# Three products of zeros added to z after each couple's sums in a graph layer kernel

## The chip, the cores and the metric

The kernel runs on one core of one Trainium2 chip. The metric is the device time of one execution in microseconds (us). The reader needs five of the core's engines: TensorE (PE in the rows, with PEld for its weight loads), VectorE (DVE), ScalarE (ACT), GpSimd (POOL, which here issues the gathers) and SyncE (SP, which issues the other DMAs).

## What is computed

The reference is one message-passing layer on a graph of 12500 nodes and 200000 edges, the edges sorted by their destination:

```python
h = jnp.maximum(_layernorm(x, axis=-1), 0.0)            # 12500 x 64
e = jnp.concatenate([h[src], h[dst]], axis=1)           # 200000 x 128
m = jax.nn.relu(e @ W1 + b1) @ W2 + b2                  # 200000 x 64
s = jax.ops.segment_sum(m, dst, num_segments=12500)
cnt = segment_sum(ones, dst)
out = x + s / jnp.maximum(cnt, 1.0)[:, None]
```

## The kernel before

A first stage of about 205 us makes two tables in DRAM: `p_table` holds the source half of `e @ W1` for each node, `q_table` the destination half plus `b1`. The second stage, `fast()`, goes over the edges. 512 edges are a quad; the first 28 quads, whose edges go to few nodes, are done in another way (below); the other 363 are taken two at a time, in 182 couples.

For a couple m, with the edges on the partitions in chunks of 128:

- POOL gathers the 1024 rows of `p_table` by `src` into a ring of 26 quads of the tile `g`, 128 rows to an indirect DMA (`gather`, L672, 8 for a couple). Before each fourth quad it waits for the semaphore `u_psum`, which counts the couples whose sums are done (L670). How many quads it may run ahead falls in five steps from 26 to 8, by 4 each 48 quads (L669, the last step by 2); at a step it has to wait for more couples than usual.
- PE puts the q rows of the edges' nodes into `z`, a PSUM tile of 128 x 1024 float32 (`spread_q`, L1374, 8 products of 128 columns), and adds the gathered rows by a product with the identity (`add_rows`, L1386, 2 products of 512 columns). Float32 products stand as two records each in the trace.
- ACT takes the relu of z back into g (`relu`, L812), which tells PE by `r_done`.
- PE sums the edges by node (`sum_edges`, L1401, 8 products of 128 columns, the last of which raises `u_psum`).
- Every couple or two `times_w2` turns the counts (L1408) and multiplies by W2 (L1419); `turn_batch` (L1430, 4 products) turns the sums of a batch of nodes, 25 times in all. DVE adds the results (L1100) and makes the means.

z is there once, so `spread_q(m + 1)` waits for the relu of m. The order on PE in the loop over m is add_rows(m), times_w2 of an earlier couple, dense(m), spread_q(m+1), sum_edges(m). `dense` is the work for the first 28 quads: six tallies a couple (L1445, bfloat16) in the couples 3 to 42, then, from couple 49 on, products of DVE on PSUM (L1153, some 7 to a couple, which read the other PSUM tile `turned`), with eight transposes on PE at the start of each of 13 spans of about 10 couples (`turn_p`, L1461).

I call a round the time from the start of one batch of 16 gathers on POOL to the start of the next; it covers two couples.

Of the kernel before, what the change touches and what calls it, by code (L numbers as in the profile page):

```python
# [14 lines left out]
NODES, FEAT, HID, EDGES = 12500, 64, 128, 200000  # L15
# [34 lines left out]
COUPLES = -(-(QUADS - Q0) // 2)  # L50
# [16 lines left out]
def couple(m):  # L67
    return range(Q0 + 2 * m, min(Q0 + 2 * m + 2, QUADS))
# [24 lines left out]
def groups_to(k):  # L93

    return sum(len(p) for p in BLOCKS[:k])
# [111 lines left out]
def gnn_kernel(nc, x, src, dst, W1, b1, W2, b2, out):  # L207
# [6 lines left out]
    with ctx:  # L214
        def sb(name, shape, dt=F32):
            return ctx.enter_context(nc.sbuf_tensor(name, shape, dt))
# [8 lines left out]
        ident = sb("ident", [128, 128])  # L225
# [3 lines left out]
        zeros = sb("zeros", [128, 128])  # L229
# [111 lines left out]
        z, turned = z_all  # L341
# [69 lines left out]
        def chunks_of(n):  # L411
            return CHUNKS - 4 * n if n == QUADS - 1 else 4
# [19 lines left out]
        def slot(n):  # L432
            return (n - Q0) % RING
# [815 lines left out]
        def _(pe):  # L1249
# [92 lines left out]
            for of, to in ((span, bank[1]), (worst, bank[2])):  # L1342
                for t in range(QT):
                    last = nc.tensor.matmul(to[0:1, 128 * t:128 * (t + 1)], of[:, t:t + 1], ident[:, :],
                                            start=True, stop=True)
# [17 lines left out]
            def spread_q(m):  # L1363

                pe.wait_ge(spread_done, parts_to(m + 1))
                if m:
                    pe.wait_ge(r_done, m)
                for n in couple(m):
                    i = GROUP[n]
                    if n == GROUPS[i][0]:  # L1370
                        pe.wait_ge(window_in[i % WINDOWS], 16 * (i // WINDOWS + 1))
                    for c in range(chunks_of(n)):
                        at = 512 * (n % 2) + 128 * c
                        last = nc.tensor.matmul(z[:, at:at + HID], spreads[m % 2][:, at:at + 128],  # L1374
                                                qw[i % WINDOWS], start=c == 0, stop=False)
                last.then_inc(zq_done, 1)
# [13 lines left out]
            def sum_edges(m):  # L1390


                pe.wait_ge(r_done, m + 1)
                if m < MEMBER_FROM:
                    pe.wait_ge(m_made, m + 1)
                k = BLOCK[m]
                for n in couple(m):
                    i = GROUP[n]
                    at = WIN * BLOCKS[k].index(i)
                    for c in range(chunks_of(n)):  # L1400
                        last = nc.tensor.matmul(u_bank[k % 2][:, at:at + WIN], g[:, slot(n), HID * c:HID * (c + 1)],  # L1401
                                                member[:, m % 2, 4 * (n % 2) + c, :], start=n == GROUPS[i][0] and c == 0,
                                                stop=n == GROUPS[i][-1] and c == chunks_of(n) - 1)
                last.then_inc(u_psum, 1)

            def turn_counts(v, parts, at):
                for j in parts:
                    nc.tensor.matmul(v[FEAT:FEAT + 1, at:at + WIN], count[:, j % COUNTS:j % COUNTS + 1], ident[:, :],  # L1408
                                     start=j == parts[0], stop=j == parts[-1])
# [12 lines left out]
            def turn_sums(i):  # L1422

                b = ORDER[i]
                if 0 < i < BATCHES - 1:
                    pe.wait_ge(mean_done, i)
                for j in range(BT):
                    t = BT * b + j
                    first = 2 * NP * (t // 2) + t % 2
                    last = nc.tensor.matmul(o_of(i)[:, j, :], sums[:, first:first + 2 * NP - 1:2], fold[:, :],  # L1430
                                            start=True, stop=True)
                last.then_inc(o_psum, 1)
# [57 lines left out]
            def fast():  # L1490
                spread_q(0)
                def turn_batch(i):
                    pe.wait_ge(v_done, groups_to(MEAN_BLOCK[ORDER[i]] + 1))
                    if ORDER[i] == 0:
                        pe.wait_ge(dense_added, 1)
                    turn_sums(i)

                for m in range(COUPLES):
                    add_rows(m)
                    if m >= 2 and m - 2 == BLOCK_END[BLOCK[m - 2]]:  # L1500
                        times_w2(BLOCK[m - 2])
                    dense(m)
                    if m + 1 < COUPLES:
                        spread_q(m + 1)
                    sum_edges(m)
                    for i in range(BATCHES):
                        if MEAN_AT[i] == m:
                            turn_batch(i)
                assert BLOCK_END[-2:] == [COUPLES - 2, COUPLES - 1]
                for k in (len(BLOCKS) - 2, len(BLOCKS) - 1):  # L1510
                    times_w2(k)
                for i in range(BATCHES):
                    if MEAN_AT[i] >= COUPLES:
                        turn_batch(i)

            def general():
# [25 lines left out]
                for i in range(BATCHES):  # L1542
                    turn_sums(i)

            if_one_window(pe, fast, general)


# [20 lines left out]
```

## Time and profile before

| | before |
|---|---|
| median of 3 runs | 2845.76 us (2832.94 to 2848.27) |
| the profiled execution | 2839.25 us, its span 2837.4 us |
| mean granted TensorE clock | 0.749 of 2.4 GHz |
| busy: PE, DVE, POOL, ACT | 55%, 50%, 48%, 42% of the span |

The span is the time from the first to the last instruction; 1.85 us of the execution lie around it. No engine is busy for much more than half of the span, so the waits between engines have to be read, not the busy times.

### The profile page before, as it was taken

How to read it: one execution, taken by the hardware profiler on the slowest of the kernel's cores; microseconds unless marked ns; L12 is line 12 of the kernel's file. 1: busy time of each engine (PE TensorE's matmuls, PEld its weight loads, DVE VectorE, ACT ScalarE, POOL GpSimd, SP SyncE). 2: the span in 40 equal slices, each digit the busy share in tenths (PEclk: the TensorE clock that was granted, in tenths of full speed). 3: DMA queues.
4: the chain of work that ended last, by engine and by line, in shares of the span. 5: the costliest groups of instructions: out<-in, count | busy, mean ns of one | idle time of the engine just before them, and what ended most of it. 6: DMA issues, size and time to landing. Idle time of an engine off the chain costs nothing.

```text
span 2837.4 us, 26976 instructions
## 1 busy us (share of the span) xinstructions
PE 1548.3 (55%) x8249; PEld 1183.2 (42%) x8250; DVE 1428.9 (50%) x3051; ACT 1189.8 (42%) x2414; POOL 1372.7 (48%) x1460
## 2 busy tenths in 40 slices
PE   1656565566465564455544555455455545555556
PEld 0545353444344443344433444344344434434444
DVE  3554343343324665456655666456565556655421
ACT  1223343444314544345444454344344444444444
POOL 6345545445555445444554435545544554554553
PEclk6878777788787777677776777767776777776778
DMA  4532222222134656556565566556565665665541
GB/s 90 163 109 60 59 61 59 60 59 58 58 98 144 202 181 189 167 169 200 179 192 154 178 188 200 186 159 183 184 192 168 186 191 174 183 186 157 174 119 43
DMA packets 258990, 408.46 MB, mean 144 GB/s; under 512 B 45128, under 2 KB 118749, under 8 KB 258841
## 3 DMA queue, kind: packets, MB, share of 16 engines
q1 hardware_dynamic: 211845, 312.84, 35.7%
q0 software_dynamic: 46432, 93.61, 12.5%
q8 instruction: 68, 1.11, 0.2%
q14 instruction: 81, 0.66, 0.1%
q10 hardware_dynamic: 564, 0.23, 0.0%
HBM read 388.12 MB, written 18.38 MB: 143 GB/s over the span
## 4 chain that ended last, share of the span: by engine, by line
PE 48%; issue 36%; another core or an unknown queue 9%; DVE 6%; ACT 1%; DMA 0%; DVEq 0%; SPq 0%; ACTq 0%
PE z L1374 16%; PE bank L1401 12%; PE z L1386 10%; DVE g L1153 4%; PE bank L1419 2%; PE bank L1408 2%; PE z L1445 2%; PE bank L1430 1%; PE z L1461 1%; DVE rows_b L936 1%; PE bank L1268 1%; DVE norms L920 1%; PE z L1268 1%; ACT g L812 0%
## 5 line engine op out<-in xcount | busy, mean ns | idle before, releaser
L672 POOL DMA_INDIRECT g<-p_table,src_e x1403 | 1326.1, 945 | 1425.3 <-PE bank L1401 960.5
L1153 DVE SCALAR_TENSOR_TENSOR g<-z,norms,g 128x1024 bf16<-128x1024 f32 (+1 forms) x884 | 1019.1, 1214 | 43.5 <-issue 25.3
L812 ACT ACTIVATE g<-z 128x1024 f32<-128x1024 f32 x182 | 185.6, 1020 | 1468.0 <-remote 1153.5
L1100 DVE TENSOR_TENSOR acc<-acc,bank 65x128 f32 x191 | 54.2, 284 | 1201.0 <-remote 1069.7
L1374 PE MATMUL z<-work 128*128 128x128 f32 x1464 | 258.8, 348 | 514.2 <-issue 482.9
L1374 PE MATMUL z<-w,work 128*128 128x128 f32 x1438 | 251.9, 345 | 484.3 <-issue 443.8
L1374 PEld LDWEIGHTS z<-work 128*128 128x128 f32 x1464 | 240.3, 256 | 546.0 <-issue 541.7
L1374 PEld LDWEIGHTS z<-w,work 128*128 128x128 f32 x1438 | 234.4, 253 | 512.3 <-issue 509.3
L1401 PE MATMUL bank<-work,g 128*128 128x128 f32 x2902 | 423.4, 307 | 15.4 <-issue 15.1
L1401 PEld LDWEIGHTS bank<-work,g 128*128 128x128 f32 x2902 | 414.1, 227 | 16.8 <-issue 16.7
L1386 PE MATMUL z<-g,ident 128*128 128x512 f32 x726 | 350.8, 605 | 5.8 <-issue 5.7
L803 ACT ACTIVATE work<-columns,rel_e 128x128 f32<-128x128 f32 x1059 | 324.2, 396 | 0.0
L1386 PEld LDWEIGHTS z<-g,ident 128*128 128x128 f32 x726 | 126.0, 194 | 98.7 <-issue 98.7
L796 ACT ACTIVATE work<-work 128x1024 f32<-128x1024 f32 (+1 forms) x168 | 146.5, 872 | 4.2
L808 ACT ACTIVATE work<-work 128x1024 f32<-128x1024 f32 (+1 forms) x133 | 140.0, 1053 | 4.2
L825 ACT ACTIVATE g<-g,norms 128x512 bf16<-128x512 f32 x157 | 108.3, 716 | 0.0
L1445 PE MATMUL z<-g 128*125 128x512 bf16 x236 | 65.6, 409 | 70.6 <-remote 67.3
L1419 PE MATMUL bank<-sums_u,w 128*64 128x128 f32 (+1 forms) x312 | 78.7, 326 | 33.3 <-issue 33.3
L830 ACT ACTIVATE g<-g 128x512 bf16<-128x512 bf16 x157 | 93.5, 620 | 0.0
L1408 PE MATMUL bank<-ident,count 128*1 128x128 f32 x432 | 74.5, 273 | 9.5 <-issue 9.4
L1408 PEld LDWEIGHTS bank<-ident,count 128*1 128x1 f32 x432 | 23.4, 81 | 128.3 <-issue 125.2
L788 ACT ACTIVATE work<-rel_q,rows_f 128x1024 f32<-128x1024 bf16 (+1 forms) x67 | 75.3, 1124 | 0.0
(161 smaller groups left out, 1063.6 us busy)
## 6 DMA issues: line engine op xcount, KB each, us to landing
g<-tally_table SPq DMA_DIRECT2D x816, 256.0 KB
rel_q<-rel_table SPq DMA_DIRECT2D x46, 512.0 KB
rows_b<-rel_table SPq DMA_DIRECT2D x45, 512.0 KB
g<-p_table,src_e POOLq DMA_INDIRECT x1403
g<-tally_table SPq DMA_DIRECT2D x68, 128.0 KB
work<-q_table SPq DMA_DIRECT2D x96, 64.0 KB
w<-q_table SPq DMA_DIRECT2D x96, 64.0 KB
g<-p_table SPq DMA_DIRECT2D x12, 512.0 KB
```

What stands on the lines that cost most here:

```text
L672: nc.gpsimd.indirect_dma_start(out=g[:, slot(n), j * HID:(j + 1) * HID], out_offset=None, in_=p_table, in_offset=bass.IndirectOffsetOnAxis ...
L796: nc.scalar.activation(to, to, ACT.Relu, bias=1.0, scale=-1.0, accum_out=count[:, j:j + 1])\
L803: last = nc.scalar.activation(member[:, m % 2, c, :], columns[:, :], ACT.Abs, bias=rel_e[:, NC + 8 * m + c:NC + 8 * m + c + 1], scale=-1.0)
L808: nc.scalar.activation(to, to, ACT.Relu, bias=1.0, scale=-1.0)
L812: nc.scalar.activation(rows_of_p(m), z[:, 0:HID * chunks_in(m)], ACT.Relu).then_inc(r_done, 1)
L1153: nc.vector.scalar_tensor_tensor(product[i % BUFFERS][:, 0:w], turned[:, 0:w], minus_q[:, d:d + 1], tally_row[i % BUFFERS][:, 0:w], ALU.ma ...
L1374: last = nc.tensor.matmul(z[:, at:at + HID], spreads[m % 2][:, at:at + 128], qw[i % WINDOWS], start=c == 0, stop=False)
L1386: last = nc.tensor.matmul(z[:, 512 * (n % 2):512 * (n % 2) + w], ident[:, :], g[:, slot(n), 0:w], start=False, stop=True)
L1401: last = nc.tensor.matmul(u_bank[k % 2][:, at:at + WIN], g[:, slot(n), HID * c:HID * (c + 1)], member[:, m % 2, 4 * (n % 2) + c, :], start ...
L1408: nc.tensor.matmul(v[FEAT:FEAT + 1, at:at + WIN], count[:, j % COUNTS:j % COUNTS + 1], ident[:, :], start=j == parts[0], stop=j == parts[-1])
L1419: nc.tensor.matmul(v_of(k)[0:FEAT, 0:w], w2[:, :], sums_u[:, k % 2, 0:w], start=True, stop=True).then_inc(v_psum, 1)
L1445: last = nc.tensor.matmul(tally_bank[i % 2][0:125, :], high_hot[p % TALLY_PLACES], low_hot[p % TALLY_PLACES], start=p == TALLY_FIRST[i], s ...
```

## The change

After `sum_edges(m)` PE makes up to three products of 512 columns that add zeros to z, which at that point holds the q part of couple m+1: the moving operand is one column of the tile `zeros`, read 512 times, the stationary one the identity. They neither wait for nor raise a semaphore of their own. Behind the last but one couple, whose successor has one quad of three chunks, they are two products of 384 columns; behind the last there are none.

```diff
+            def add_nothing(m):
+                if m + 1 == COUPLES:
+                    return
+                for k in range(3):
+                    at = 512 * (k % 2)
+                    w = min(512, HID * chunks_of(couple(m + 1)[k % 2])) if k % 2 < len(couple(m + 1)) else 0
+                    if w:
+                        nc.tensor.matmul(z[:, at:at + w], ident[:, :], zeros[:, 0:1].to_broadcast([128, w]),
+                                         start=False, stop=False)
...
                     if m + 1 < COUPLES:
                         spread_q(m + 1)
                     sum_edges(m)
+                    add_nothing(m)
                     for i in range(BATCHES):
                         if MEAN_AT[i] == m:
                             turn_batch(i)
```

PE's instructions of two couples in the stage with tallies, before. For each: q part into z (L1374), sums (L1401), gathered rows of the next couple into z (L1386), then tallies (L1445) or counts and W2 (L1408, L1419).

```order
L1374 MATMUL z<-w,work 128x128 x8
L1401 MATMUL bank<-work,g 128x128 x8
L1386 MATMUL z<-g,ident 128x512 x2
L1445 MATMUL z<-g 125x512 x6
L1374 MATMUL z<-w,work 128x128 x8
L1401 MATMUL bank<-work,g 128x128 x8
L1386 MATMUL z<-g,ident 128x512 x2
L1408 MATMUL bank<-ident,count 1x128 x2
L1419 MATMUL bank<-sums_u,w 64x128
```

Two such couples on PE after the change; lines behind the new function have numbers that are 10 higher.

```order
L1374 MATMUL z<-w,work 128x128 x8
L1401 MATMUL bank<-work,g 128x128 x8
L1413 MATMUL z<-zeros,ident 128x512 x3
L1386 MATMUL z<-g,ident 128x512 x2
L1455 MATMUL z<-g 125x512 x6
L1374 MATMUL z<-w,work 128x128 x8
L1401 MATMUL bank<-work,g 128x128 x8
L1413 MATMUL z<-zeros,ident 128x512 x3
L1386 MATMUL z<-g,ident 128x512 x2
L1418 MATMUL bank<-ident,count 1x128 x2
L1429 MATMUL bank<-sums_u,w 64x128
```

The zeros (L1413) stand between the sums and the gathered rows of the next couple; nothing else has moved, on this engine or another.

## Rows read from the trace of the kernel before

**Rows 1.** The page: totals, slices, and shares of the chain that ended last.

```profile
PE 1548.3 (55%) x8249; PEld 1183.2 (42%) x8250; DVE 1428.9 (50%) x3051; ACT 1189.8 (42%) x2414; POOL 1372.7 (48%) x1460
...
PEclk6878777788787777677776777767776777776778
...
PE 48%; issue 36%; another core or an unknown queue 9%; DVE 6%; ACT 1%; DMA 0%; DVEq 0%; SPq 0%; ACTq 0%
```

**Rows 2.** Waits, all engines: waiter, releaser, us in total, times, longest.

```profile
ACT g L812 <- remote: 1153.5, 83, 15.6
POOL g L672 <- PE bank L1401: 960.5, 84, 27.9
```

**Rows 3.** Timeline, 1500 to 1560: start, length, what; [idle before].

```profile
1503.90 0.94 POOL L672 DMA_INDIRECT g<-p_table,src_e  x1 [11.01 <-PE bank L1401]
...
1508.36 1.95 PE L1401 MATMUL bank<-work,g 128*128 128x128 f32 x16
1510.15 1.88 PE L1386 MATMUL z<-g,ident 128*128 128x512 f32 x4
...
1512.27 0.43 PE L1419 MATMUL bank<-sums_u,w 128*64 128x128 f32 x2
...
1522.62 0.94 POOL L672 DMA_INDIRECT g<-p_table,src_e  x1 [0.30 <-issue]
1526.70 1.02 ACT L812 ACTIVATE g<-z 128x1024 f32<-128x1024 f32 x1 [14.50 <-remote]
...
1527.82 3.75 PE L1374 MATMUL z<-w,work 128*128 128x128 f32 x16 [15.12 <-issue]
1531.37 2.96 PE L1401 MATMUL bank<-work,g 128*128 128x128 f32 x16
1534.60 0.94 POOL L672 DMA_INDIRECT g<-p_table,src_e  x1 [11.03 <-PE bank L1401]
...
1536.08 1.02 ACT L812 ACTIVATE g<-z 128x1024 f32<-128x1024 f32 x1 [2.56 <-PE z L1386]
1537.20 2.02 PE L1374 MATMUL z<-w,work 128*128 128x128 f32 x16 [0.49 <-issue]
```

**Rows 4.** Windows: sum, busy of PE, PEld, DVE, ACT, POOL, clock, DMA, GB/s.

```profile
1516.00:1519.00 3.00, 0.00 (x0) 0.00 (x0) 0.00 (x0) 0.00 (x0) 2.09 (x4) 0.57 0.81 273
1527.00:1531.00 4.00, 3.18 (x15) 3.21 (x16) 3.54 (x6) 3.97 (x11) 0.00 (x0) 0.50 0.16 53
```

**Rows 5.** Timeline of PE and POOL, a round with eight L1461 and L1430 records more.

```profile
998.84 0.94 POOL L672 DMA_INDIRECT g<-p_table,src_e  x1 [10.97 <-PE bank L1401]
...
1005.39 0.88 PE L1430 MATMUL bank<-fold,acc 65*125 65x65 f32 x6
...
1015.87 0.45 PE L1419 MATMUL bank<-sums_u,w 128*64 128x128 f32 x1 [0.37 <-issue]
...
1029.55 0.94 POOL L672 DMA_INDIRECT g<-p_table,src_e  x1 [11.05 <-PE bank L1401]
```

**Rows 6.** POOL's waits for the sums, 230 to 900, and the start of one batch.

```profile
POOL g L672 <- PE bank L1401: 215.1, 22, 24.6
...
841.28 0.94 POOL L672 DMA_INDIRECT g<-p_table,src_e  x1 [3.49 <-remote]
```

**Rows 7.** The same from 960 to 2800, and the starts of batches behind two steps of the lead.

```profile
POOL g L672 <- PE bank L1401: 684.2, 59, 25.7
...
1701.64 0.94 POOL L672 DMA_INDIRECT g<-p_table,src_e  x1 [24.45 <-PE bank L1401]
2077.24 0.94 POOL L672 DMA_INDIRECT g<-p_table,src_e  x1 [17.77 <-PE bank L1401]
```

**Rows 8.** Timeline: a restart of PE after a short pause, and the clock there (windows).

```profile
853.14 2.77 PE L1374 MATMUL z<-work 128*128 128x128 f32 x16 [3.67 <-issue]
...
853.00:854.00 1.00, 0.86 (x8) 0.89 (x9) 0.00 (x0) 1.00 (x2) 0.70 (x2) 1.00 0.11 29
```

**Rows 9.** Timeline of PE: the end of the program.

```profile
2825.01 0.81 PE L1386 MATMUL z<-g,ident 128*128 128x384 f32 x2
```

## The prediction

> **What bounds the kernel now.** I read the page first. No engine is busy for much over half of the span, and the chain that ended last is 48% PE and 36% "issue", time in which an engine waits for nothing that the profile shows [rows 1]. So the waits decide. They say that two engines wait for each other: POOL waits for PE's sums for 960.5 us in 84 waits, and ACT's relu waits for z for 1153.5 us in 83 [rows 2].
>
> The timeline shows how that can be [rows 3]. Take the round that starts on POOL at 1503.90. The last of its 16 gathers is issued at 1522.62 and ends at 1523.56. ACT's relu starts at 1526.70, 3.14 later, PE's q part at 1527.82, the sums at 1531.37, and the next batch at 1534.60. So a round is 19.66 (gathers) + 3.14 + 1.12 (relu) + 3.55 (q part) + 3.23 (sums) = 30.70 us, for two couples.
>
> What is the relu waiting for? The product that it needs, L1386, has its record at 1510.15, 1.88 long, so it seems done at 1512.03, yet the relu begins 14.67 us later. In the next couple, right after a batch has started, the same relu follows promptly: PE's sums are in by about 1534.3 and the relu starts at 1536.08. I read this so: from about 3 us after a batch starts until 3.1 us after its last gather, PE's records run on, but what PE has done is told to the others only slowly, and the rest in one go at the end. Where the delay sits I can't see; that ACT calls its releaser "remote" only says that the profile has no better name. Call the couple whose sums start a batch A and the one behind it B. A's q part and sums lie in the open, between the landing and the next batch. B's are all issued by 1512.70 (the row of 1512.27 with its 0.43), and PE then idles for 15.12 us. The clock has fallen meanwhile: 0.57 in 1516 to 1519, 0.50 in 1527 to 1531 [rows 4]. So A's q part takes 3.75 us for its 16 records where B's takes 2.02, and its sums 2.96 where B's take 1.95 [rows 3].
>
> **The price of the zeros.** Two products of 512 columns are four records in 1.88 us at the high clock [rows 3]; three are 2.8, less the overlap of their ends; I take 2.7. At the low clock it would be twice as much, 5.4. With 182 couples all of them in the open would cost 180 x 2.7 = 490 us at the high clock, 970 at the low one; nothing if all are covered. They use no other engine and raise no semaphore, so only PE's own order matters: what comes behind them is `add_rows` of the next couple, and behind that its relu.
>
> *A's zeros.* They stand behind `u_psum`, so the batch at 1534.60 doesn't wait for them. `add_rows` ends at 1538.7 instead of 1536.0. That lies past the 3 us in which PE is heard at once, so the relu may come another 1 to 3 us later, and B's q part starts about 1541 to 1543 instead of 1537.20.
>
> *B's zeros.* B's work then ends 2.7 + 2.7 + (1 to 3) = 6.4 to 8.4 us later than before: 1512.70 becomes 1519.1 to 1521.1 in the round shown. The relu is not released before 1526.70 anyway, so 5.6 to 7.6 us are left. The cover is POOL's batch; with it gone each round would cost the 5.4. A natural trial is in the trace: the round from 998.84 has eight L1461 records and eight L1430 records more, is issued only by 1016.3 (1015.87 + 0.45), 17.5 us after its start instead of 8.8, and the next batch still starts at 1029.55, 30.71 us after it [rows 5]. So from 960 on, where 56 of the 59 waits are of one kind, (684.2 - 25.7 - 24.5 - 17.8) / 56 = 11.0 us each [rows 7], I cost the zeros at nothing, but for some five rounds in which they meet both L1461 and L1430: 5 us in all, bounds 0 and 15 (three us each).
>
> *The clock.* With the zeros PE is idle for 15.12 - 6.4 to 8.4 = 6.7 to 8.7 us before the restart. Before, the clock was at half speed by 1519, 6.3 us after the last record [rows 4]. So it has fallen again before A's q part, and A costs what it did. A warm restart exists: at 853.14, after 3.67 us of idling, the clock reads 1.00 and the q part takes 2.77 [rows 8]. The pause would have to shrink to something like that.
>
> **What is not covered.** (a) At a step of POOL's lead two more couples (at the last step one) have to be summed with no gathers under way: the batches at 1701.64 and 2077.24 waited 24.45 and 17.77 us instead of 11.0 [rows 7]. There is one such wait before 900 (24.6, [rows 6]), two more of over 23 and one of 17.8 behind it. PE is then busy in every couple, and zeros lie on the path twice in four of the steps and once in the fifth: 9 x 2.7 = 24 us.
> (b) The start: before the first gated batch the zeros of couple 0 lie on the path, 2.7 us.
> (c) The end: no gathers are left, and the zeros after three couples are in the open; the last of them are two products of 384 columns, 0.81 each [rows 9]: 2.7 + 2.7 + 1.6 = 7 us.
> (d) Rounds before 900 are often shorter. 21 of the 22 waits there, without the long one, average (215.1 - 24.6) / 21 = 9.07 us, and one more is 3.49 [rows 6]; 11.0 is the value of the late ones. In such a round PE is through, and heard, before the end of the batch. With 6.4 to 8.4 us more of PE it is not, and the round becomes a long one. If all became so: 21 x (11.0 - 9.07) + (11.0 - 3.49) = 48 us; if none, 0. I take 29, 0.6 of it, because the long rounds are not all at 11.0 there and those without tallies keep some slack.
>
> **Sum.** 24 + 2.7 + 7 + 29 + 5 = 68 us. On the profiled execution's 2839.25 (span 2837.4 and 1.85 around it) that is 2907; the median of the runs, 2845.76, lies 6.5 higher, which gives 2914. I say 2910. The bounds of the unknown terms, (d) 0 to 48 and the five rounds 0 to 15, give 2877 to 2942, so 2872 to 2945 is the forecast's own range.
>
> **Rivals.** *The clock stays up (faster).* The zeros shorten PE's pause before A. If A's q part and sums ran at the high clock, a round would save (3.75 - 2.02) + (2.96 - 1.95) = 2.7 us, over the 84 rounds 230 us; with the 68 that gives 2845 - 230 + 68, about 2683. It pays from 68 / 2.7 = 25 warm rounds on; with half of them warm it is 2800. For it: the restart at 853.14 [rows 8]. Against it: a pause of 6.7 to 8.7 us remains where 6.3 saw the clock down. By the Trainium skill (TensorE: Matmul & The Clock Gate, the table under "Why this matters for your kernels") throughput drops when TensorE pauses between bursts, so padding of this kind can pay; by that rule alone, if the padding closes the pause, the time would be this rival's 2683. The trace agrees as far as it goes: a high clock behind the pause of 3.67 us, a low one behind 15.12.
>
> *The cover is too short (much slower).* If A's `add_rows`, now beyond the 3 us, is told not 1 to 3 but 10 us late, as everything later in a batch is, B's relu and sums end about 1529, behind the release, and up to 2.7 us of zeros lie open in each of the 84 rounds: + 227, about 3140 with the 68; half of it about 3025. For it: nothing in the trace puts a relu just there. Against it: [rows 5]. It decides once the relu of B starts more than about 12 us after the batch.
>
> *Covered everywhere (no change).* If (a) is covered too, or the 29 and half of the rest fall away, under 14 us remain: 2850. Against it: in (a) and (c) there is nothing to cover them.
>
> **Numbers.** My forecast 0.60; too short a cover 0.20; clock stays up 0.12; no change 0.08. About 0.5%, 14 us, is what a measurement of this kernel tells from no change. Faster by more: 0.10 (a few warm rounds would only cancel the 68). Within: 0.10. Slower: 0.80. For 8 in 10 the range reaches from 2848 over my own range to 2995, which takes in the milder half of the cover's rival.
>
> **What would show it.** Rounds from 960 on still 30.7 long, with an 11.0 wait on POOL; the relu behind A's zeros 4.2 to 7.2 us after the batch's start instead of 1.5 (1534.60 to 1536.08); PE's longest pause 15 down to 7 to 9 us; A's q part still 3.75 long; mean clock up from 0.749 to about 0.85, with no gain; waits before 900 near 10.5; the five long ones 30 and 20 instead of 24 and 18. Wrong, if A's q part takes near 2 us in many rounds (then faster), or if POOL's waits grow beyond 12 from 960 on (then the cover is too short).

## The result

| | before | with the zeros |
|---|---|---|
| median of 4 runs each, same chip | 2845.85 us (2832.94 to 2848.27) | 2902.38 us (2899.91 to 2909.92) |
| the profiled execution, its span | 2837.4 us | 2898.6 us |
| mean granted clock | 0.749 | 0.834 |

The change is slower: ratio 1.0209, 95% interval 1.0188 to 1.0230. The page of the changed kernel, the rows that answer to [rows 1]:

```profile
PE 2048.3 (71%) x9333; PEld 1343.7 (46%) x9334; DVE 1430.5 (49%) x3051; ACT 1190.6 (41%) x2414; POOL 1376.9 (48%) x1460
...
PEclk9878888888887888788888888888887878878879
...
PE 55%; issue 27%; another core or an unknown queue 9%; ACT 7%; DVE 1%; DMA 0%; SPq 0%; DVEq 0%; ACTq 0%
```

PE is busy for 500 us more and the span is 61 us longer, so most of the zeros are indeed covered. The waits, all engines, as in [rows 2] (waiter, releaser, us in total, times, longest):

```profile
POOL g L672 <- PE bank L1401: 1017.8, 85, 34.7
ACT g L812 <- remote: 795.9, 64, 17.5
```

POOL's wait has grown from 960.5 to 1017.8, by 57.3 us: nearly the whole loss passes through it. The same wait in the two stretches of [rows 7] and [rows 6], 960 to 2860 and then 230 to 930:

```profile
POOL g L672 <- PE bank L1401: 712.9, 60, 30.8
...
POOL g L672 <- PE bank L1401: 248.8, 22, 29.9
```

Where the 61.2 us are, read from the starts of POOL's batches in the two timelines (us; a step is the one round in which the lead falls):

| | before | after | difference | predicted |
|---|---|---|---|---|
| up to the first gated batch | 223.2 | 228.6 | +5.4 | +2.7 |
| 22 rounds before 930, without the step | 626.6 | 663.5 | +36.9 | +29 |
| the five steps | 214.7 | 237.0 | +22.3 | +24 |
| 54 rounds behind them, without the steps | 1654.6 | 1635.4 | -19.2 | +5 |
| the last three rounds | 92.2 | 103.0 | +10.8 | in the +5 |
| behind the last batch | 26.1 | 31.3 | +5.2 | +7 |

(They add up to 61.4 by rounding.)

The late rounds did not stay as they were, they gave 19 us back. The timeline of the changed kernel shows how one of them goes, the round that starts on POOL at 1587.48 (start, length, what; in brackets the idle time before and what ended it):

```profile
1587.48 0.95 POOL L672 DMA_INDIRECT g<-p_table,src_e  x1 [10.41 <-PE bank L1401]
...
1589.63 1.88 PE L1386 MATMUL z<-g,ident 128*128 128x512 f32 x4
...
1591.54 1.02 ACT L812 ACTIVATE g<-z 128x1024 f32<-128x1024 f32 x1 [4.48 <-issue]
...
1596.31 2.75 PE L1413 MATMUL z<-zeros,ident 128*128 128x512 f32 x6
...
1600.29 0.22 PE L1440 MATMUL bank<-fold,acc 65*125 65x65 f32 x1 [0.71 <-issue]
1602.43 0.22 PE L1440 MATMUL bank<-fold,acc 65*125 65x65 f32 x1 [1.92 <-issue]
1605.22 0.27 PE L1440 MATMUL bank<-fold,acc 65*125 65x65 f32 x1 [2.57 <-issue]
1607.31 1.01 PE L1386 MATMUL z<-g,ident 128*128 128x512 f32 x1 [1.83 <-issue]
1608.72 2.72 PE L1386 MATMUL z<-g,ident 128*128 128x512 f32 x3 [0.40 <-issue]
...
1612.60 2.18 PE L1374 MATMUL z<-w,work 128*128 128x128 f32 x16
...
1616.84 0.95 POOL L672 DMA_INDIRECT g<-p_table,src_e  x1 [9.65 <-PE bank L1401]
```

Three things are to be seen. The relu behind A's zeros comes 4.06 us after the batch (1587.48 to 1591.54), instead of 1.48 us: by the length of the zeros and no more. The record of A's `add_rows` ends at 1591.51 (1589.63 + 1.88), so the relu follows at once, and it does so in all 53 such rounds between 960 and 2720. The further delay of 1 to 3 us that the prediction added did not come. From 1600 on PE's records come one at a time, 1.4 to 2.8 us apart, although nothing that the profile shows holds them (I call this a trickle): that was not in the prediction. And A's q part, behind PE's work without a pause, takes 2.18 us instead of 3.75. In 18 of the 56 rounds whose batch starts between 960 and 2720 most of A's q part ran at the high clock; before it was 3 of 57, the steps.

### The profile page after: what moved, and what is told of

It is laid out like the page before. It is cut to its first block, busy times and chain, and to the rows that moved or that the text cites. A ratio compares the mean times of both kernels' runs of the same rounds, so it can differ in the third digit from the quotient of the medians.

```text
span 2898.6 us, 29144 instructions
## 1 busy us (share of the span) xinstructions
PE 2048.3 (71%) x9333; PEld 1343.7 (46%) x9334; DVE 1430.5 (49%) x3051; ACT 1190.6 (41%) x2414; POOL 1376.9 (48%) x1460
## 4 chain that ended last, share of the span: by engine, by line
PE 55%; issue 27%; another core or an unknown queue 9%; ACT 7%; DVE 1%; DMA 0%; SPq 0%; DVEq 0%; ACTq 0%
PE z L1413 13%; PE z L1374 13%; PE z L1386 10%; PE bank L1401 10%; ACT g L825 3%; PE bank L1429 3%; PE bank L1418 2%; ACT g L830 2%; ACT g L812 1%; PE bank L1440 1%; DVE rows_b L936 1%; PE z L1455 0%; DVE norms L920 0%; PE z L1471 0%
## 5 line engine op out<-in xcount | busy, mean ns | idle before, releaser
L672 POOL DMA_INDIRECT g<-p_table,src_e x1403 | 1330.2, 948 | 1477.0 <-PE bank L1401 1017.8
L1413 PE MATMUL z<-zeros,ident 128*128 128x512 f32 x1084 | 504.3, 596 | 31.1 <-issue 30.8
L1386 PE MATMUL z<-g,ident 128*128 128x512 f32 x726 | 383.8, 643 | 58.4 <-issue 58.2
L1401 PE MATMUL bank<-work,g 128*128 128x128 f32 x2902 | 386.6, 290 | 3.3 <-issue 3.2
L1401 PEld LDWEIGHTS bank<-work,g 128*128 128x128 f32 x2902 | 375.6, 209 | 5.0 <-issue 5.0
L1374 PE MATMUL z<-work 128*128 128x128 f32 x1464 | 242.5, 332 | 127.8 <-issue 121.9
L1374 PE MATMUL z<-w,work 128*128 128x128 f32 x1438 | 238.0, 331 | 116.6 <-issue 105.7
L1374 PEld LDWEIGHTS z<-work 128*128 128x128 f32 x1464 | 225.2, 242 | 174.5 <-issue 170.4
L1374 PEld LDWEIGHTS z<-w,work 128*128 128x128 f32 x1438 | 221.7, 241 | 163.9 <-issue 162.9
L1413 PEld LDWEIGHTS z<-zeros,ident 128*128 128x128 f32 x1084 | 192.9, 191 | 206.3 <-issue 206.0
L1386 PEld LDWEIGHTS z<-g,ident 128*128 128x128 f32 x726 | 144.6, 201 | 249.8 <-issue 249.5
L1429 PE MATMUL bank<-sums_u,w 128*64 128x128 f32 (+1 forms) x312 | 92.2, 356 | 154.5 <-issue 154.5
L1418 PE MATMUL bank<-ident,count 128*1 128x128 f32 x432 | 91.6, 292 | 88.4 <-issue 88.3
L1455 PE MATMUL z<-g 128*125 128x512 bf16 x236 | 88.5, 475 | 77.3 <-issue 52.0
L1429 PEld LDWEIGHTS bank<-sums_u,w 128*64 128x64 f32 x312 | 36.8, 148 | 182.1 <-issue 181.4
```

Source lines behind the costliest of these rows:

```text
L672: nc.gpsimd.indirect_dma_start(out=g[:, slot(n), j * HID:(j + 1) * HID], out_offset=None, in_=p_table, in_offset=bass.IndirectOffsetOnAxis ...
L1386: last = nc.tensor.matmul(z[:, 512 * (n % 2):512 * (n % 2) + w], ident[:, :], g[:, slot(n), 0:w], start=False, stop=True)
L1413: nc.tensor.matmul(z[:, at:at + w], ident[:, :], zeros[:, 0:1].to_broadcast([128, w]), start=False, stop=False)
L1429: nc.tensor.matmul(v_of(k)[0:FEAT, 0:w], w2[:, :], sums_u[:, k % 2, 0:w], start=True, stop=True).then_inc(v_psum, 1)
```

## The experiments

The ratios are to runs of the kernel before on the same chip. The runs came from three chips: the kernel before took 2845.21 us beside the first four, 2827.68 beside the next four, 2843.54 and 2846.84 beside the rest. So spans are compared inside one group only. Late rounds can be compared across groups: from 950 to 2060 the kernel before agrees with itself to 0.1 us. Early rounds can't without a control, and the runs that change only late couples serve as one: on the chip of the first four the 22 early rounds without the step take 628 and 632 us there, on the chip of the next four 611, 618 and 613, in the two profiles of the kernel before 627 and 625.

### Early or late

The zeros in two halves. Late, in the couples that something covers:

```diff
-                if m + 1 == COUPLES:
+                if m + 1 == COUPLES or not (49 <= m < 171 and m not in (51, 52, 77, 78, 103, 104, 129)):
```

> Three products of zeros, as in the change, but only behind the couples 49 to 170 without the seven whose zeros lay open at POOL's steps (51, 52, 77, 78, 103, 104, 129): 115 couples. Cover theory: the gathers hide them, and where PE's pause shrinks enough the q part behind it starts at the high clock; the stretches between the steps then give back what they gave in the changed kernel (337.5 to 336.5, 337.0 to 328.8, 338.2 to 330.5, 641.9 to 639.6 us), 19 us, so 2827 us, ratio 0.993 (0.985 to 1.0). Rival, every product costs alike: 115 of 181 couples' share of the 61 us, + 39 us, ratio 1.014.

Measured: 2838.26 us, ratio 0.9974 (0.9957 to 0.9992), span 2829.3. The late half alone is a gain. 19 of 57 of A's q parts are at the high clock.

Early, before couple 49:

```diff
-                if m + 1 == COUPLES:
+                if m + 1 == COUPLES or not (m < 49):
```

> The zeros only behind the couples 0 to 48, where PE also has the tallies and POOL waits in many rounds less than 11 us. Cover theory: these carry the start (+5), the step in that stretch (+5) and the rounds that were short and become long (+37): + 47 us, 2893 us, ratio 1.0165 (1.012 to 1.021). Rival, every product costs alike: 49 of 181 couples, + 17 us, ratio 1.006.

Measured: 2890.52 us, ratio 1.0144 (1.0118 to 1.0171). Some 45 of the loss of 57 us come from the 49 early couples, and their rounds before 930 are as long as with the whole change (331.1 and 334.9 us without the step; 329.6 and 333.9 with the change; 315.5 and 311.1 before, and 314.3 and 313.9 on the chip of this run with the late zeros alone). Term (d) is where I had it. Its reason is not, as the next run shows.

### The same number of products, next to no time

```diff
-                        nc.tensor.matmul(z[:, at:at + w], ident[:, :], zeros[:, 0:1].to_broadcast([128, w]),
+                        nc.tensor.matmul(z[:, at:at + 1], ident[:, :], zeros[:, 0:1],
```

> The same number of products in the same places, but one column each instead of up to 512: the instructions stay, their streaming time goes (2.7 us to some 0.2 a couple). Theory that PE's time is what costs: no change from before, 2845 us, ratio 0.999 to 1.003, since neither the steps nor the end get longer and the pauses stay as they were. Rival, it is the number of instructions that have to be told one by one while gathers land: the short rounds before 900 us still become long, + 15 to 40 us, ratio 1.005 to 1.014.

Measured: 2883.51 us, ratio 1.0116 (1.0082 to 1.0150). The rounds before 930 are again long: 330.7 and 334.8 us. PE is busy for only 1702.9 us there, so it isn't PE's time that (d) pays for, but the number of its instructions, or something that goes with it. The steps, where I had counted time, grow little here: 220.9 us for the five, where the whole change has 237.0 and the kernel before 214.7. The timelines of one short round, first of the kernel before (its second profile, e9 below, on another chip), then of the one with one column, from the start of the batch:

```profile
282.49 0.94 POOL L672 DMA_INDIRECT g<-p_table,src_e  x1 [10.71 <-PE bank L1401]
...
291.13 0.43 PE L1420 MATMUL bank<-sums_u,w 128*64 128x128 f32 x2
291.49 1.51 PE L1446 MATMUL z<-g 128*125 128x512 bf16 x6
300.95 1.02 ACT L812 ACTIVATE g<-z 128x1024 f32<-128x1024 f32 x1 [11.27 <-remote]
...
307.50 0.95 POOL L672 DMA_INDIRECT g<-p_table,src_e  x1 [5.32 <-PE bank L1401]
```

```profile
288.99 0.94 POOL L672 DMA_INDIRECT g<-p_table,src_e  x1 [10.42 <-PE bank L1401]
...
298.96 0.43 PE L1429 MATMUL bank<-sums_u,w 128*64 128x128 f32 x2
299.32 0.78 PE L1455 MATMUL z<-g 128*125 128x512 bf16 x2
300.40 0.38 PE L1455 MATMUL z<-g 128*125 128x512 bf16 x1 [0.29 <-issue]
...
303.24 0.38 PE L1455 MATMUL z<-g 128*125 128x512 bf16 x1 [0.83 <-issue]
311.83 1.02 ACT L812 ACTIVATE g<-z 128x1024 f32<-128x1024 f32 x1 [14.98 <-remote]
...
319.35 0.94 POOL L672 DMA_INDIRECT g<-p_table,src_e  x1 [10.69 <-PE bank L1401]
```

PE's work ends 10.5 us after the batch's start in the one (293.00) and 14.6 in the other, far ahead of the relu in both. But in the second the last tallies trickle, and the relu comes 22.8 us after the batch's start instead of 18.5; the round is 30.4 long instead of 25.0. Counted over the rounds of this run before 900, where there is a trickle it begins, mostly, when 61 or 62 product records have followed the batch's start, some ten of them the tallies' bfloat16 ones; later, where nearly all are float32, mostly at 51 to 57. The count alone doesn't fix the relu, though: in the early rounds of the kernel before, with 52 to 58 product records in a round's gathers, the relu comes anywhere from 17.0 to 22.9 us after the batch's start.

### Six one-column records a round

```diff
-                if m + 1 == COUPLES:
+                if m + 1 == COUPLES or not (m < 49 and m % 2 == 0):
...
+                        nc.tensor.matmul(z[:, at:at + 1], ident[:, :], zeros[:, 0:1],
```

> Three products of one column each (six records of nearly no length) behind the sums of couple B only, in the couples before 49; nothing elsewhere. Theory N, the number of PE's instructions between the start of the batch and the last one that the others wait for makes a short round a long one: with one column behind all couples the short rounds before 900 cost 38 us (315.5 to 330.7 and 311.1 to 334.8), and as what stands ahead of A's next relu is the same three products, B's alone cost as much when the delay sits there: + 30 to 38 us, span 2867 to 2875, ratio 1.011. If the delay comes from A's products (ahead of B's relu): + 0 to 8, ratio 1.000 to 1.003. Half each: + 15 to 20, ratio 1.006. Theory T, PE's time: 0.

Measured: 2859.62 us, ratio 1.0111 (1.0096 to 1.0127), span 2857.9. Three products of one column behind every second early couple, about 25 couples, cost 32 us (2859.62 less 2827.68), most of the 38 of the run above. They are 0.7 us of PE in a round. A theory in which PE's time counts can't give that. The rounds agree with the span: before 930, without the step, they take 327.7 and 318.8 us, and 303.4 and 307.3 in the run with A's late zeros alone, on the same chip. And the trickle is not what makes the relu late: in the 18 rounds from 249.7 to 837.7 without the step, all 58 or 62 product records run on without one and are through 10.3 to 11.5 us after the batch's start, and the relu still comes 21.8 to 22.7 us after it. Only the two rounds from 837.7 on, with 50 records, stay short (23.1 and 24.8 us).

### A larger dose

Six products behind each of the late covered couples (`range(6)`, the late condition).

> Six products instead of three behind the same 115 couples as in the run that has three there. Cover theory: the second couple of a round ends another 5 to 8 us later, at about its release, 0 to 3 us of it in the open; PE's pause is gone, so nearly all q parts start at the high clock and save up to 2.5 us. The two about cancel: 2790 to 2850 us, ratio 0.98 to 1.0, with q parts of 2 us in over 40 of the 57 rounds. If the cover had been much longer, the ratio would be near 0.95; if it was already used up with three, 57 x 5.4 = 308 us more, ratio 1.10.

Measured: 2977.02 us, ratio 1.0442 (1.0411 to 1.0473), clock 0.847. Nearly every q part of A was now at the high clock (51 of 52), and the rounds were still 2 us longer than before: with some 70 records in a round more trickles, and what trickles lies in the open (A's q part starts 9.7 us after the last gather on average instead of 5.1). So the second rival of the prediction, too short a cover, is real, but not by its mechanism: the relu behind A's six products is not told late. It comes 6.65 us after the batch in most rounds, 0.04 us behind the record of `add_rows`. What uses up the cover is the trickle behind it.

### Only A's, only B's

The late condition, and for A `(m % 2 == 1) == (m < 130)`, for B `(m % 2 == 0) == (m < 130)`.

> The zeros stand only behind the sums of couple A (those that release the batch), and only in the covered couples from 49 on, about half of those of the run with both couples' zeros (span 2829.3 against 2837.4, 19 of 57 q parts of A begun at the high clock). Theory 1, it is the length of PE's pause before A's q part that counts: A's zeros push everything of B back by 2.7 us and the relu behind them by up to 3 more, so the pause shortens by 4 to 6 us, most of what both did (6.5): 10 to 15 warm q parts, span 2830 to 2835, ratio about 0.998. Theory 2, it is what PE does last before the pause that counts: A's zeros stand too early, few q parts are warm (under 6), and the late relu of B costs nothing: span 2835 to 2840, ratio 0.999 to 1.001. If the late relu were itself the cost, it would show here as rounds over 30.8 us.

> The zeros stand only behind the sums of couple B, in the covered couples from 49 on. They delay no relu that anyone waits for. Theory 1 (length of the pause): the pause shortens by only 2.7 us, to about 12.4: no more q parts are warm than before (3 of 57), span 2836 to 2840, ratio 1.000. Theory 2 (what PE does last before the pause): as many warm q parts as with both, 15 to 20, span 2829 to 2832, ratio 0.997.

Measured: A's alone 2808.53 us, ratio 0.9931 (0.9917 to 0.9945), span 2800.7; B's alone 2816.66 us, ratio 0.9960 (0.9948 to 0.9973), span 2814.7. Both theories miss: few q parts are at the high clock (6 and 4, the three at the steps among them), about as theory 1 has it for B and theory 2 for A, and yet both runs gain. A's alone gains 19 us, clearly more than the two together (0.9974, 0.9957 to 0.9992); for B's alone the intervals overlap. The rounds say how. In the run with A's zeros most last 30.7 us, but here and there one lasts 29 and the next ones 29.7, 30.2, 30.5, 30.6. One event shortens five rounds. That asked for another theory of what a round's length is.

### Zeros inside the pause

Nothing in z; six products in `times_w2`, where it follows A's gathered rows, into the bank that the result goes to next:

```diff
+                for _ in range(busy):
+                    nc.tensor.matmul(bank[6][:, :], ident[:, :], zeros[:, 0:1].to_broadcast([128, 512]),
+                                     start=True, stop=True)
...
-                        times_w2(BLOCK[m - 2])
+                        times_w2(BLOCK[m - 2], 6 if 49 <= m < 171 and (m % 2 == 1) == (m < 130) else 0)
```

> No zeros in z. Where the counts and W2 of a block follow A's gathered rows, PE makes six products of 512 columns of zeros into the bank of that block's result before it, 5.4 us of PE inside its pause; they stand behind the product that the relu waits for, so no relu is late. Theory 1 (length of the pause): the pause shortens by 5.4 to about 9.7 us in the rounds that have such a block, as many or nearly as many warm q parts as with the change's own late zeros (15 to 19 of 57), and nothing given back: span 2825 to 2832, ratio 0.995 to 0.998. Rival: the warm q parts with the zeros in z came from the later start of B's q part and sums, not from busy PE; then this one changes nothing: span 2836 to 2840, ratio 1.000, under 6 warm.

Measured: 2821.84 us, ratio 0.9985 (0.9970 to 0.9999), span 2818.3. In between: the same single short rounds appear, but I had not left out the couples at the steps, whose rounds grew by 4.7 us each (48.4, 49.9, 48.8 and 42.0 instead of 43.6, 45.3, 44.1 and 37.4). Without these 19 us it would be near the run with A's zeros alone; that was not run.

### What a round's length is

The kernel before, once more (with an empty line added, so its later lines have numbers one higher), and one product put on the path itself, between A's q part and A's sums:

> The kernel before itself, for a second profile of it beside the next two. All theories: ratio 1.000 within 0.002. What it is to show: whether the rounds between the steps last 30.7 us again where the times of another chip are lower by half a per cent, that is, whether 30.7 is a sum of gathers and waits (then it moves with them) or is held by something else.

```diff
+            def add_nothing(m):
+                if 49 <= m < 171 and m not in (51, 52, 77, 78, 103, 104, 129) and (m % 2 == 1) == (m < 130):
+                    nc.tensor.matmul(z[:, 0:512], ident[:, :], zeros[:, 0:1].to_broadcast([128, 512]),
+                                     start=False, stop=False)
...
                         spread_q(m + 1)
+                    add_nothing(m)
                     sum_edges(m)
```

> No zeros behind the sums. One product of 512 columns of zeros (two records) into z between A's q part and A's sums, in the covered couples from 49 on, about 55 of them: on the very path that releases the batch. Theory S, the one of my prediction: a round is the sum 19.66 + 3.14 + 1.12 + 3.55 + 3.23, so each such round grows by the product, 0.94 us at the high clock and 1.9 at the low one: + 52 to + 105 us, ratio 1.018 to 1.037, rounds of 31.6 to 32.6. Theory L: the clock rises at a moment of its own that does not move with the restart of PE, so work added ahead of the release only shortens what is done at the low clock; the time from A's q part to the batch stays near 6.8 and the rounds stay 30.7: span within 5 us of before, ratio 0.998 to 1.002. A round that is disturbed comes back to 30.7 in halves.

Measured: before again 2844.28 us, ratio 1.0006 (0.9987 to 1.0025). With the product 2853.53 us, ratio 1.0043 (1.0028 to 1.0057), span 2850.6 against 2839.3. 58 products on the path, 1.0 to 1.9 us long each and most of them 1.1, cost 11 us and not 54 or more; behind the first rounds of a stretch every round is 30.7 us again. Theory S, the sum of my prediction, is refuted; L missed its band of 5 us by 6, of which below.

Windows of 2 us in the kernel before (its second profile), laid 30.72 us apart within two stretches: two where all is regular, four where it is disturbed. Behind the sum stand the busy times of PE, PEld, DVE, ACT and POOL, then the clock:

```profile
1505.39:1507.39 2.00, 2.00 (x14) 1.97 (x14) 2.00 (x5) 1.18 (x3) 0.00 (x0) 0.75 0.88 246
1536.11:1538.11 2.00, 2.00 (x14) 1.95 (x14) 2.00 (x5) 1.15 (x2) 0.00 (x0) 0.75 0.76 198
...
2351.90:2353.90 2.00, 2.00 (x15) 2.00 (x15) 2.00 (x3) 1.97 (x6) 0.00 (x0) 0.75 0.00 0
2382.62:2384.62 2.00, 2.00 (x15) 2.00 (x15) 2.00 (x5) 1.97 (x3) 0.00 (x0) 0.75 0.91 202
2413.34:2415.34 2.00, 2.00 (x15) 2.00 (x15) 2.00 (x3) 1.97 (x4) 0.00 (x0) 0.75 0.83 277
2444.06:2446.06 2.00, 2.00 (x16) 2.00 (x15) 2.00 (x5) 1.97 (x5) 0.00 (x0) 0.75 1.02 286
```

0.75 in a window is half of it at 0.5 and half at 1.0: the clock rises in the middle of each. So the rises are 30.72 us apart, in the disturbed stretch as in the regular one. A's q part and POOL's batches are not. The timeline of that stretch:

```profile
2350.85 2.05 PE L1374 MATMUL z<-w,work 128*128 128x128 f32 x8
2355.91 0.95 POOL L672 DMA_INDIRECT g<-p_table,src_e  x1 [9.47 <-PE bank L1401]
2379.92 2.05 PE L1374 MATMUL z<-work 128*128 128x128 f32 x8 [14.77 <-issue]
2385.76 0.95 POOL L672 DMA_INDIRECT g<-p_table,src_e  x1 [10.15 <-PE bank L1401]
2409.74 2.05 PE L1374 MATMUL z<-w,work 128*128 128x128 f32 x8 [14.74 <-issue]
2416.01 0.94 POOL L672 DMA_INDIRECT g<-p_table,src_e  x1 [10.54 <-PE bank L1401]
2440.14 2.05 PE L1374 MATMUL z<-work 128*128 128x128 f32 x8 [13.69 <-issue]
2446.56 0.94 POOL L672 DMA_INDIRECT g<-p_table,src_e  x1 [10.85 <-PE bank L1401]
```

From A's q part to the rise (the middle of the window) it is 2.05 us at 2352.90, then 3.70, 4.60 and 4.92, and 5.4 to 5.7 in the regular rounds. The rise doesn't wait for the q part: it comes at its own moment, and the earlier PE restarts, the more of its work runs at half speed. A restart that is d earlier therefore ends only d/2 earlier, and the next round starts from that: the lead halves from round to round until the round is 30.72 us again. That is the 29.2, 29.9, 30.2, 30.5, 30.6 of this stretch (2326.74 to 2355.91, to 2385.76, and so on). The shortenings add up to 3.2 us over these five, and a single event of the run with A's zeros (28.5, 30.1, 30.4, 30.6, 30.6 from 984.4 on) comes to about as much. Here the event was a round with L1462 (`turn_p`), in which PE was at work until 2350.80 and the rise came sooner than its place in the series, 27.3 us behind the one before it.

The changed kernel shows the same. Behind a round whose q part ran at the high clock, its rounds from 1082.83 on last 30.2, 30.4, 30.6, 30.6 and 30.7 us, and its windows 1110.21:1112.21, 1140.93:1142.93, 1171.65:1173.65 and 1202.37:1204.37, again 30.72 us apart, all read a clock of 0.76. From 960 to 2735 its trace has 56 distances from one rise to the next: 37 are 30.7 us, ten are shorter (27.3, one 23.9), five are 34.1, and four, at the steps, longer still; the kernel before has 52 of 30.7, one of 27.3 and the three at the steps. So the late rounds gained where a rise came sooner than its place, and lost some of it where one came later.

In the run with a product ahead of the sums, two windows and two rounds of one stretch:

```profile
1385.35:1387.35 2.00, 2.00 (x9) 1.19 (x9) 2.00 (x5) 1.87 (x3) 0.00 (x0) 0.75 0.59 200
1569.67:1571.67 2.00, 2.00 (x10) 1.52 (x10) 2.00 (x5) 1.97 (x3) 0.00 (x0) 0.75 0.60 199
```

```profile
1381.55 3.75 PE L1374 MATMUL z<-work 128*128 128x128 f32 x16 [15.15 <-issue]
1385.10 1.65 PE L1408 MATMUL z<-zeros,ident 128*128 128x512 f32 x2
...
1388.80 0.94 POOL L672 DMA_INDIRECT g<-p_table,src_e  x1 [11.54 <-PE bank L1401]
...
1566.94 3.75 PE L1374 MATMUL z<-w,work 128*128 128x128 f32 x16 [12.31 <-issue]
1570.48 1.12 PE L1408 MATMUL z<-zeros,ident 128*128 128x512 f32 x2
...
1573.66 0.94 POOL L672 DMA_INDIRECT g<-p_table,src_e  x1 [11.07 <-PE bank L1401]
```

The windows are six rounds apart, 184.32 us. The q part has moved from 4.80 us ahead of the rise to 3.73, and the batch comes 6.72 us after it, as in [rows 3] (6.78), with the product in between. What the added work took, the shorter time at the low clock gave. The 11 us that L did not expect are the way there (rounds of 31.7, 31.2, 30.9 behind one step) and the short event near 2350, which no longer occurs.

### Filling the pause

Products of zeros just ahead of A's q part, into a bank of sums that is free at the time:

```diff
+            def keep_busy(m):
+                if not (49 <= m < 171 and m not in (51, 52, 77, 78, 103, 104, 129) and (m % 2 == 1) == (m < 130)):
+                    return
+                k = BLOCK[m] + (m - 1 != BLOCK_END[BLOCK[m - 1]])
+                for _ in range(12 - 8 * any(SPAN_FIRST[i] - 1 in (m - 1, m) for i in range(SPANS)) - 2 * (m - 1 in MEAN_AT)):
+                    nc.tensor.matmul(u_bank[k % 2][:, :], ident[:, :], zeros[:, 0:1].to_broadcast([128, 512]),
+                                     start=True, stop=True)
...
                     dense(m)
+                    keep_busy(m)
```

> No zeros in z. In the covered A couples from 49 on PE makes up to twelve products of 512 columns of zeros (11.3 us at the high clock) into the bank of sums that is free at that time, behind A's gathered rows and whatever counts, W2 and transposes follow them, so inside the pause of 15.1 us before A's q part; four where transposes fill it already, two less behind a batch of means. Nothing that another engine waits for stands behind them but A's q part, which waits for the relu anyway. Theory W (a short pause keeps the clock up, and a q part and sums at the high clock take 4.1 us instead of 6.8): 30 to 55 warm q parts, rounds near 28.0, - 80 to - 140 us, ratio 0.95 to 0.972. Rival 1 (the remaining pause of 4 us or so is enough for the clock to fall again): as before, ratio 0.998 to 1.002. Rival 2 (more PE instructions while gathers land make the relu before the q part later, as in the early rounds with one column): rounds over 31, ratio over 1.005.

Measured: 2905.95 us, ratio 1.0208 (1.0174 to 1.0243). All three theories miss. Most q parts are at the high clock, and rounds of 28.0 occur, as theory W has it, but others last 32 to 34. The relu is not late, which refutes rival 2. The timeline from the batch at 1134.8 on:

```profile
1143.57 2.85 PE L1411 MATMUL bank<-zeros,ident 128*128 128x512 f32 x6
1146.96 0.59 PE L1411 MATMUL bank<-zeros,ident 128*128 128x512 f32 x1 [0.54 <-issue]
...
1155.48 1.01 PE L1411 MATMUL bank<-zeros,ident 128*128 128x512 f32 x1 [0.41 <-issue]
1156.88 7.61 PE L1411 MATMUL bank<-zeros,ident 128*128 128x512 f32 x12 [0.39 <-issue]
1164.33 1.95 PE L1374 MATMUL z<-work 128*128 128x128 f32 x16
```

At 1143.57 the zeros run on at full speed, six records; then one comes each 1.4 to 2.1 us; at 1156.88 the rest is there at once, twelve records in 7.61 us, and A's q part starts at 1164.33, where the relu was through at 1158.76. In the round from 1106.9 the same 24 records fit (16 ran on at full speed) and the round took 28.0. Over this run's late rounds the trickle begins mostly at 51 to 57 product records behind the batch's start, in six rounds at 58 or 59, in three at 62 or 63 and in two at 50, and 8.5 to 17.1 us after it. The changed kernel is tighter: in 49 of its 53 late rounds it begins at 54 to 56 records, 11.4 to 16.4 us into the batch. (I count up to the first idle time of over 0.2 us that lies more than 7 us into the batch.) So a count fits and a time doesn't. The instruction queues of the profile (q8 and q14) are no explanation: in the round from 2184.9 of the changed kernel no packet of theirs runs from the batch's start to 2206, and the trickle begins at 56 records all the same; 14 of the 53 rounds are like it.

The last run keeps the fill within that count: seven products, five from couple 150 on, three less behind a batch of means, none next to the transposes, and none in the couples 51, 53, 77, 79, 103, 105, 129 and 130:

```diff
+                for _ in range((7 if m < 150 else 5) - 3 * (m - 1 in MEAN_AT)):
```

> The pause of A filled as in the run with twelve products, but with seven (five from couple 150 on, three less behind a batch of means), none next to the transposes and none in the eight couples that lie open at the steps. In that run PE's product records ran on at full speed until 51 to 62 of them had followed the start of the batch, then came one at a time, 0.6 to 2.8 us apart, until some 3 us behind the last gather; what was left of the twelve products then lay in the open and made A's q part 2 to 6 us late. Theory stock (PE has a limited number of instructions at hand when gathers begin): seven products, 14 records behind the 44 of a plain round, use up the stock and the slow arrivals and leave little in the open; PE is still at work just before A's q part in many rounds, so 15 to 35 q parts at the high clock, those rounds near 28, steps back at 44 and 37: span 40 to 90 us under before, ratio 0.970 to 0.988. Rival: the fill costs by its time, not by its number of instructions, and what is not covered stays so in part: ratio 0.995 to 1.01.

Measured: 2825.09 us, ratio 0.9930 (0.9908 to 0.9952), span 2821.1. The steps are back at 44 and 37, and little is left in the open: A's q part starts 5.2 us after the last gather on average, before 5.1. But the gain is a quarter to a little over half of what I expected, and only 8 of 57 q parts are at the high clock. The timeline of a typical round:

```profile
2139.72 2.85 PE L1411 MATMUL bank<-zeros,ident 128*128 128x512 f32 x6
...
2151.63 1.01 PE L1411 MATMUL bank<-zeros,ident 128*128 128x512 f32 x1 [0.27 <-issue]
...
2155.00 3.75 PE L1374 MATMUL z<-work 128*128 128x128 f32 x16 [2.36 <-issue]
```

The pause is 2.36 us, and the q part is at the low clock all the same: a PE that trickles, one record in 0.7 to 2.1 us, has lost the clock already. The window 2143:2145 still reads 1.00, 2147:2149 reads 0.50, and until then no pause of PE in this trickle was over 0.81 us. In the next round eight transposes trickle until 0.68 us before the q part, which again takes 3.75. In the changed kernel all 18 q parts at the high clock follow a pause of 0.5 us or less.

## Why the prediction was right, and where not

It forecast 2910 us (2848 to 2995), slower; it is 2902.38. Point by point:

- **What the page and the waits say, and who A and B are**: stood. The loss passes through POOL's wait.
- **(a) The steps**, 24 us: 22.3, or 2.5 for each of the nine places. (c) **The end**, 7: 5.2. Both as the prediction had them. The one-column run, where the steps grow by only 6.2, bears out that time is the price there. (b) **The start**, 2.7: 5.4, which can't be told from the spread: where nothing early is changed, the first gated batch starts anywhere from 221.7 (the run with a product ahead of the sums) to 228.8 (the kernel before again).
- **(d) Short rounds**, 29 us: 36.9, the size within its bounds and the waits as forecast ((248.8 - 29.9) / 21 = 10.42, "near 10.5"). The step behind it failed: I wrote that PE is through "before the end of the batch", and with 6.4 to 8.4 us more of PE it is not. The one-column runs show that 0.7 us of PE in a round does the same. What counts is the number of instructions or what goes with it, and why the relu then waits for the gathers is open.
- **A's zeros and the late relu**: the length of the zeros stood, the extra 1 to 3 us did not. The relu comes 4.06 us after the batch, just under the 4.2 to 7.2 forecast, 0.03 us behind `add_rows`. So PE is heard at once beyond the first 3 us, up to 6.65 us in the run with six products, and B's work ends later by the two lots of zeros alone, some 5.3 us and not 6.4 to 8.4. It cost nothing in the sum, since the cover was not used up by time.
- **"A's q part costs what it did"**, with the pause down to 6.7 to 8.7 us: this is the step that was wrong in part. Where a pause was left (27 of 56 rounds, 3.1 to 8.1 us) it held: the q part began at the low clock. But in the other 29, the three steps among them, under 2 us were left, mostly filled by trickling, and in 18 of these the q part ran at the high clock. The rival had its mechanism but not its price. It counted 2.7 us for each warm round, 40 us for the 15 that are more than before. The late rounds gave back 19.2, since a round is held to 30.72 us by the clock's rises, and a gain is spent again over the next rounds. The changed kernel's rises, 37 of 56 of them 30.7 us apart, bear that out; how much each late round with trickling work in the open took back was not separated.
- **The round as a sum**, 19.66 + 3.14 + 1.12 + 3.55 + 3.23: right as arithmetic, wrong as a cause. A product put ahead of the sums is a term more, and the sum did not grow.
- **Five rounds at 5 us**: mis-sized. The last three rounds alone grew by 10.8: those of 32.1 and 31.0 us became 37.3 and 35.5. Part of it is again number and not time: with one column the same two take 36.1 and 34.2, against 32.1 and 33.0 on the same chip with the early zeros alone. Of the rival with too short a cover the six products showed the whole, and the last three rounds of the changed kernel are likely its beginning; that was not tried.
- **The bounds of the sum**, 2877 to 2942, mix two bases: 33.7 and 96.7 us give 2873 to 2936 on the profiled execution and 2879 to 2942 on the median. The range wasn't affected.

The forecast came close partly by luck, because errors met: the late rounds are 24 us under what I had, (b), (d) and the last rounds 21 over it, (a) and (c) 4 under.

By the Trainium skill (TensorE: Matmul & The Clock Gate, the table under "Why this matters for your kernels") idle gaps of TensorE between bursts lower its throughput, so filling them should pay. The trace agrees that q parts run faster behind it, and shows that it pays little here: 0.7% at the best of five placements, and a loss where the added instructions meet the gathers.

## What to carry to other kernels

Added TensorE work that looks covered has two prices, its time where nothing covers it and its number of instructions while gathers are under way; make the same instructions of one column and see which of the two you pay. Where rounds keep the same length to 0.1 us although their content differs, suspect that something outside the work sets it: add a known piece to the path and see whether the sum grows. And zeros behind A's sums alone, in couples that gathers cover, beat both kernels (2808.53 us, 0.9931), as do seven inside the pause (0.9930); behind every couple they lose.

## What the runs showed of the hardware

- While POOL's indirect gathers are under way, PE runs on for mostly 51 to 57 float32 product records (each with its weight load) from the batch's start, and then gets them one at a time, 0.6 to 2.8 us apart. In the changed kernel this began at 54 to 56 records in 49 of 53 late rounds, and 11.4 to 16.4 us into the batch, so by count. With six products it ended 2.3 to 3.1 us after the last gather. Whether it is the supply of instructions was not shown; no packet of an instruction queue goes with it in 14 of the 53 rounds.
- Such a trickle doesn't hold the clock: it fell from 1.00 to 0.50 between 2145 and 2147 in the last run with no pause over 0.81 us, and a q part took 3.75 us 0.68 us behind the last of eight trickling records.
- In the kernel before, the granted clock's rises before A's sums end were 30.72 us apart through regular and disturbed rounds alike, but for one that came after 27.3 us and those at the steps. They did not follow PE's restart, which lay 2.05 to 5.7 us ahead of them.
